# Routing stage of a mixture-of-experts kernel: four input blocks and twelve weight buffers in place of two and four, four weight parts split between the norm's steps

## The reference, cut to what matters

```
xn = (x - mean) / sqrt(var + 1e-5)
attn: v = xn @ Wv.T; r = sigmoid(xn @ Wr.T); wkv = scan over time with decay and first   # no k in it
      (r * wkv) @ Wo.T
ffn:  scores = softmax(xn @ gate_w.T + gate_b)           # 8 experts
      top_w, top_i = top_k(scores, 2)
      y = sum over the 2 chosen experts e of top_w * ((silu(xn @ w1[e].T + b1[e]) * (xn @ w3[e].T + b3[e])) @ w2[e].T + b2[e])
      z = (silu(xn @ ws1.T + bs1) * (xn @ ws3.T + bs3)) @ ws2.T + bs2
out = x + attn(xn) + y + z
```

## Time and profile before

| | |
|---|---|
| median of three runs | 557.25 us (554.65 to 558.19) |
| profiled execution | 556.1 us, span 554.0 us |
| PE busy | 471.2 us (85%) |
| DVE busy | 435.1 us (79%) |
| ACT busy | 234.7 us (42%) |
| POOL busy | 266.9 us (48%) |
| `route` | 0 to 102.4 us of the span |
| first gather of `run_experts` | 102.7 us |

### The profile page before, as it was taken

One profiled execution on the slowest core, in us unless ns is written; L12 is line 12 of the kernel. 1 busy time (PEld: TensorE's weight loads), 2 busy tenths in 40 slices (PEclk: granted clock), 3 DMA queues, 4 the chain that ended last, 5 costly groups with the idle time before them and its releaser, 6 DMA issues. The chain is left out here.

```text
span 554.0 us, 10837 instructions
## 1 busy us (share of the span) xinstructions
PE 471.2 (85%) x2624; PEld 381.1 (69%) x2625; DVE 435.1 (79%) x963; ACT 234.7 (42%) x535; POOL 266.9 (48%) x312
## 2 busy tenths in 40 slices
PE   0668027499999999999999995989999999999997
PEld 0333013188878777777878784777889888988887
DVE  7877869357888888877888873899979696887974
ACT  0335334136656565555655563342232323242321
POOL 6000000353666666666565654878683754657300
PEclk9999555589999999999999998999999999999999
DMA  2798344138434333333333333924471817163111
GB/s 78 258 316 310 122 142 147 28 107 267 124 106 125 111 120 116 114 110 117 104 114 114 104 96 115 321 77 131 125 204 45 236 46 211 58 188 96 58 38 39
DMA packets 58553, 73.95 MB, mean 133 GB/s; under 512 B 6848, under 2 KB 47552, under 8 KB 58528
## 3 DMA queue, kind: packets, MB, share of 16 engines
q1 hardware_dynamic: 52048, 55.94, 30.8%
q0 software_dynamic: 6480, 17.70, 12.0%
HBM read 45.39 MB, written 28.18 MB: 133 GB/s over the span
## 5 line engine op out<-in xcount | busy, mean ns | idle before, releaser
L858 POOL DMA_INDIRECT xg<-xn_rows,picked x71 | 71.1, 1002 | 57.6 <-POOL picked L855 33.3
L1343 POOL DMA_INDIRECT yg<-expert_rows,rows x64 | 72.2, 1128 | 23.6 <-issue 17.1
L855 POOL COPY picked<-tile_tok 128x1 int32 (+1 forms) x71 | 13.9, 196 | 97.8 <-POOLq L315 93.2
L922 PE MATMUL ps_g<-w_hi,x_hi 128*128 x142 | 57.2, 403 | 0.9 <-DVE x_lo L1077 0.9
L922 PE MATMUL ps_g<-w_lo,x_hi 128*128 x142 | 56.6, 398 | 0.0
L922 PE MATMUL ps_g<-w_hi,x_lo 128*128 x142 | 56.5, 398 | 0.0
L1374 PE MATMUL ps_w<-col_hi,s_hi 128*128 128x512 f32 x128 | 51.1, 399 | 1.3 <-DVE res L1569 0.9
L1151 DVE RECIPROCAL rden<-den 128x128 f32<-128x128 f32 x32 | 30.3, 948 | 26.5 <-POOL den L872 26.5
L1375 PE MATMUL ps_w<-col_lo,s_hi 128*128 128x512 f32 x128 | 50.2, 392 | 0.0
L1376 PE MATMUL ps_w<-col_hi,s_lo 128*128 128x512 f32 x128 | 50.2, 392 | 0.0
L995 ACT ACTIVATE act<-ps_g 128x256 f32<-128x256 f32 x71 | 27.2, 383 | 52.0 <-PE ps_g L925 48.5
(11 more groups left out here) (199 smaller groups left out, 1421.8 us busy)
## 6 DMA issues: line engine op xcount, KB each, us to landing
expert_rows<-y SPq DMA_DIRECT2D x71, 128.0 KB
table<-mix_tables SPq DMA_DIRECT2D x16, 384.0 KB
raw_s<-x SPq DMA_DIRECT2D x16, 256.0 KB, 3.7
col<-xn_columns SPq DMA_DIRECT2D x8, 512.0 KB, 7.4
mix_tables<-coef SPq DMA_DIRECT2D x16, 256.0 KB
res<-x SPq DMA_DIRECT2D x16, 256.0 KB
out<-res SPq DMA_DIRECT2D x16, 256.0 KB
xn_rows<-raw_s SPq DMA_DIRECT2D x8, 256.0 KB, 3.7
```

The source lines that it names most:

```text
L858: pool.indirect_dma_start(out=xg[a.buf(NG)][:], out_offset=None, in_=xn_d[:, :], in_offset=bass.IndirectOffsetOnAxis(ap=picked[a.buf(NG)][ ...
L922: nc.tensor.matmul(out, x[:, k, :], w[:, ds(e, 1), k, cols].rearrange("p o n -> p (o n)"), start=(k == 0 and n == 0), stop=False)
L1343: pool.indirect_dma_start(out=yg[a.buf(2)][:, k, q, :], out_offset=None, in_=y_d[:, :], in_offset=bass.IndirectOffsetOnAxis(ap=picked[a.bu ...
```

## The change

- `route` gets buffers of its own: four for `xin` (NX = 4), two for `xn`, two for `xT`, four more of 128 x 768 floats named `w_soon`, and seven for the maps of the choice. The memory of the later stages is allocated after `route` has freed its own, from the other side of SBUF.
- SP loads the first four x blocks at once and behind them weight parts 0 to 3 into `w_soon`. In steps 0 to 3 it loads x block i+4 once `xn` of step i is written; in steps 4 to 7 it loads weight parts 4 to 7 into `xin` buffers that are free by then. Parts 8 and 9 go to `xn`, 10 and 11 to `xT`, 12 to 15 to `w_soon` again.
- ACT clears `bias_hl` in eight pieces of 128 x 768, one after the copies of each step, in place of the memset of POOL.
- DVE does `measure` of step i+1 before `norm` of step i, and splits parts 0 to 3 after the norms of steps 4 to 7; ACT splits them in steps 2 to 5.
- The slot loop has one split per batch on DVE, and one on ACT in its first four batches, behind `hot_tok` and not ahead of it.
- The loops of hardware (`Fori`) in `route` are written out.

```diff
-            w_hi = sb("w_hi", [P, E, KC, WALL], F32R, experts)
...
+            y = [sb(f"y{b}", [P, C], F32, experts, "right") for b in range(2)]
+            w_hi = sb("w_hi", [P, E, KC, WALL], F32R, experts, "right")
...
-        xin = [spare_x[:, b, :].rearrange("p (q c) -> p q c", q=Q) for b in range(2)]
-        xn = [spare_n0, spare_n1[:].rearrange("p k n -> p (k n)").rearrange("p (q c) -> p q c", q=Q)]
-        xT = [spare_t, sb("xT1", [P, KC, STEP], F32)]
-
-        NW = 4
-        w_raw = [t[:].rearrange("p k n -> p (k n)")[:, 0:WALL] for t in (spare_n0, spare_n1, *xT)]
+        NX = 4
+        xin = [sb(f"xin{b}", [P, Q, C], F32) for b in range(NX)]
+        xn = [sb(f"xn{b}", [P, Q, C], F32) for b in range(2)]
+        xT = [sb(f"xT{b}", [P, KC, STEP], F32) for b in range(2)]
+
+        SOON = 4
+        NW = SOON + NX + 4
+        w_soon = [sb(f"w_soon{b}", [P, WALL], F32) for b in range(SOON)]
+        w_raw = ([t[:] for t in w_soon]
+                 + [t[:].rearrange("p k n -> p (k n)")[:, 0:WALL] for t in (*xin, *xn, *xT)])
...
@@ SyncE @@
-                load_x(At(0, 1, 2))
+                for i in range(1, NX):
+                    load_x(At(0, i, NSTEP))
+                for i in range(SOON):
+                    load_w(i)
+
+                def step(a):
+                    sp.wait_ge(s_xn, a.i + 1)
+                    if a.i + NX < NSTEP:
+                        load_x(a.plus(NX))
...
+                    if a.i + NX >= NSTEP:
+                        load_w(SOON + a.i + NX - NSTEP)
...
-                with sp.Fori(1, E * KC // NW) as u:
-                    for r in range(NW):
-                        load_w(At(u, r, NW))
+                for i in range(NW, E * KC):
+                    load_w(i)
...
@@ GpSimd @@
-                nc.gpsimd.memset(bias_hl[:].rearrange("h e n -> h (e n)").bitcast(F32), 0.0).then_inc(s_bzero, 1)
...
@@ ScalarE @@
+                    nc.scalar.activation(bias_hl[:, a.i, :].bitcast(F32), ident[:, 0:1].broadcast_to([P, WALL]),
+                                         ACT.Copy, scale=0.0).then_inc(s_bzero, 1)
...
+                for i in range(1, NSTEP - 2):
+                    step(At(0, i, NSTEP))
+                    if i > 1:
+                        split(i - 2)
...
+                split(SOON)
+                split(SOON + 1)
                 exps(1, EARLY, NSTEP)
-                half = E * KC // 2
-                for n in range(half):
-                    split(At(0, n, half))
+                for i in range(SOON + 2, NW):
+                    split(i)
                 for n in range(PAIRS // BATCH):
-                    if n < half:
-                        split(At(1, n, half))
...
+                    if NW + n < E * KC:
+                        split(NW + n)
...
@@ VectorE @@
+                measure(At(0, 0, NSTEP))
+                for i in range(NSTEP):
+                    if i + 1 < NSTEP:
+                        measure(At(0, i + 1, NSTEP))
+                    norm(At(0, i, NSTEP))
+                    if i > 1:
+                        take(At(0, i - 2, NSTEP))
+                    if i >= NSTEP - SOON:
+                        split(i - NSTEP + SOON)
...
                 for n in range(EARLY, NSTEP):
-                    take(At(n // 2, n % 2, 2))
+                    if n >= NSTEP - 2:
+                        take(At(0, n, NSTEP))
                 choose(1, EARLY, NSTEP)
...
-                split(0)
-                split(1)
+                split(SOON)
+                split(SOON + 1)
...
-                split(2)
+                split(SOON + 2)
+                split(SOON + 3)
...
-                SPLIT_AFTER = [(3, 4), (5, 6), (7,), (8,), (9, 10), (11, 12), (13,), (14, 15)]
+                SPLIT_AFTER = [(8,), (9,), (10,), (11,), (12,), (13,), (14,), (15,)]
```

More of the change, by code:

```diff
@@ new lines, in build @@
+            w_hi = sb("w_hi", [P, E, KC, WALL], F32R, experts, "right")
+            w_lo = sb("w_lo", [P, E, KC, WALL], F32R, experts, "right")
+            bias_hl = sb("bias_hl", [P, E, WALL], F32R, experts, "right")
+            ones2 = sb("ones2", [P, P], F32R, experts, "right")
+            route(nc, x, first, decay, vec_tf, vec_td, gate_w, gate_b, w_all, b_all, xn_d, xT_d, ident, slots, gates,
+                  tile_tok, tile_exp, w_hi, w_lo, bias_hl, ones2)
+            raw_s13 = sb("raw_s13", [P, KC, 2 * SF], F32)
@@ new lines, in build @@
+            raw_s2 = sb("raw_s2", [P, KS, C], F32)
+            raw_o = sb("raw_o", [P, KC, C], F32)
+            vr_hi, vr_lo = (sb(f"vr_{s}", [P, KC, 2 * C], F32R) for s in ("hi", "lo"))
+            col0 = sb("col0", [P, KC, STEP], F32)
+            col_hi0 = sb("col_hi0", [P, KC, STEP], F32R)
+            col_lo0 = sb("col_lo0", [P, KC, STEP], F32R)
+            vec_b1 = sb("vec_b1", [P, KS], F32)
+            vec_b3 = sb("vec_b3", [P, KS], F32)
+            row_b2 = sb("row_b2", [P, C], F32)
@@ L174, in build @@
+            raw_vr = sb("raw_vr", [P, KC, 2 * C], F32, experts, "right")
+            run_experts(nc, xn_d, y_d, y, y_stored, tab_d, vec_tf, vec_td, ident, tile_tok, tile_exp, w_hi, w_lo, bias_hl,
                         ones2,
@@ L188, in route @@
 def route(nc, x, first, decay, vec_tf, vec_td, gate_w, gate_b, w_all, b_all, xn_d, xT_d, ident, slots, gates,
-          tile_tok, tile_exp, w_hi, w_lo, bias_hl, ones2, spare_x, spare_n0, spare_n1, spare_t):
+          tile_tok, tile_exp, w_hi, w_lo, bias_hl, ones2):
     with ExitStack() as ctx:
@@ L230, in route @@
         logits = sb("logits", [P, NT, E], F32)
[L231 to L234, removed]
+        score = maps[0][:].rearrange("p (j e) -> p j e", e=E)
+        work = maps[1][:].rearrange("p (j e) -> p j e", e=E)
+        work2 = maps[2][:].rearrange("p (j e) -> p j e", e=E)
+        hot = [maps[3 + k][:].rearrange("p (j e) -> p j e", e=E) for k in range(TOPK)]
         red = sb("red", [P, NT], F32)
@@ L273, in route @@
         s_small = sem("s_small")
-        s_xin = [sem(f"s_xin{b}") for b in range(2)]
+        s_xin = [sem(f"s_xin{b}") for b in range(NX)]
         s_w = [sem(f"s_w{b}") for b in range(NW)]
@@ L740, in _, with run_experts @@
                                         ).then_inc(s_tok, 1)
-def run_experts(nc, xn_d, y_d, y_stored, tab_d, vec_tf, vec_td, ident, tile_tok, tile_exp, w_hi, w_lo, bias_hl, ones2,
+def run_experts(nc, xn_d, y_d, y, y_stored, tab_d, vec_tf, vec_td, ident, tile_tok, tile_exp, w_hi, w_lo, bias_hl, ones2,
                 cuts, loads):
@@ L765, in run_experts @@
         h_lo = [sb(f"h_lo{b}", [P, KC, P], F32R) for b in range(2)]
-        y = [sb(f"y{b}", [P, C], F32) for b in range(2)]
         s_p = sb("s_p", [P, KC, PIECE + 1], F32)
```

150 lines of the change are left out of this document (42 added, 108 removed).

## The result

The changed kernel takes 569.39 us (median of 4 runs, 568.1 to 571.75), the kernel before in the same job 556.44 us (median of 4 runs, 554.65 to 558.19): a ratio of 1.0238 with a 95% interval of 1.0186 to 1.0289. Forecast were 541 us and a range of 535 to 548. The profiled execution took 570.31 us (before 556.1) with a span of 568.6 us (before 554.0) and a mean granted clock of 0.919 (before 0.941).

A forecast was written before the change was run, and what follows sets the result against it. `route` was taken to set the end, since the first gather waits for its barrier. Start -4.6, norm -1.4, choice and places +0.1, slot loop -10.0 sum to -15.9 us: 541 us, range 535 to 548.

The forecast's parts named there:

- What bounds the kernel: The first gather waits for the barrier behind `route`, so each microsecond by which `route` ends earlier comes off the end.
- Part 1: Start of `route`: without POOL's memset DVE's cast is faster, first BN_STATS at 6.0 in place of 10.62 us, -4.6 us.
- The bound of 0: Start of `route`: no gain, first BN_STATS still at 10.6 us, if the cast is slow for a reason besides the memset.
- Part 2: Norm in `route`: choice starts at 42.7 in place of 48.67 us, -6.0 us, of which 4.6 come from the start.
- one `take` 0.2 us: Norm, DVE's time per step: the copy of logits priced at 0.2 us, six of them in a 40.7 us total.
- the chain from the end of `norm` i over ACT, 5.5 us: Norm: transposes, gate product, logits, piece, split and root take 5.5 us; `norm` i+2 starts about 7 us later, 1.5 spare.
- The transfers of Part 2: Norm, one queue: 11.9 MB ahead of the `xn` store of step 5, 34.6 us at 341 to 345 GB/s; done by 39.4.
- Part 3: Choice to slot loop: earlier `take` saves 0.75 us, one more split costs 0.87, net +0.1; loop starts at 65.4 us.
- Part 4: Slot loop: eight batches with one split each on DVE take 20.4 in place of 30.4 us, -10.0 us.
- The rivals: Norm gains nothing (0.17, 547 us); better case (0.14, 537 or 538); PE at low level (0.04, 566); change hidden (0.03, 557).
- PE falls to its low level: Norm: PE's clock drops between waits for transfers, steps take 7.2 us against 4.1, kernel at 566 us; chance 0.04.
- the signs of being wrong: Clock of 0.5 across the norm, `norm` waiting for `xn_rows` over 2 us in most steps, or other durations after the barrier.

The follow-up runs named there:

- the first experiment: The changed kernel with DVE copying the logits of step i-3, not i-2, after the norm of step i: 540.41 us, ratio 0.971 to the kernel before.
- the last: The first experiment with each `xn` store issued ahead of the next x block and split 3 ahead of the norm's last `take`: 538.20 us, ratio 0.9656.
- the experiment on the memset: The first experiment with `bias_hl` cleared by one memset on POOL again, not by eight pieces on ACT: 544.54 us in one run.

## Why the prediction was wrong

- **What bounds the kernel: right.** `route` sets the end: the span moved with the first gather, by +14.6 us for +13.83 in the change, -15.0 for -15.28 in the first experiment and -15.4 for -16.91 in the last, whose profiled execution was the slowest of its six (540.31 us).
- **Part 1: right.** First BN_STATS at 5.89 us, forecast 6.0. The bound of 0, a cast that is slow for another reason, fell with the experiment on the memset.
- **Part 2: the step that failed is "one `take` 0.2 us".** I priced the moved `take` by its duration and gave it no wait. It waits 5.4 us on average (32.5 / 6), and `norm` of the next block, on which PE waits, stands behind it. I had seen that the change calls `take(i-2)`, and named it a gain: "releases the `back` of step 7 earlier". I went through the chain from the end of `norm` i over ACT, 5.5 us, and compared it with the start of `norm` i+2. That holds for ACT, but asks nothing of DVE's own waits: the logits of i-2 stand on PE behind the transposes of i and the gate product of i-1, and their reader now stands between `norm` i and `norm` i+1. The waits of before don't name it, as `take` of i-3 waited 2.0 us in all. But its price stood in the earlier trace rows, once the two programs are laid side by side: transposes and gate product 1.09 + 1.88 us, and 0.66 us for `back`, which the same trace has on PE though no row of mine showed it. That is 3.6 us, the wait measured at the high level (3.59 us).
- **The transfers of Part 2: right, as soon as the wait is gone.** In the first experiment the norms start at 10.12, 13.66, 18.89, 23.60, 27.54, 32.05, 36.55 and 39.02 us, forecast 10.2, 13.9, 18.6, 23.1, 27.7, 32.5, 37.3 and 40.0, and the choice at 42.49, forecast 42.7. That the choice agrees to 0.2 us is partly luck: the last norm came 1.0 us early, and a wait of 1.12 us for PE ahead of the last `take`, which the forecast lacked, made up for it. The rate of 345 GB/s was set too low: 362 to 379 were reached.
- **Part 3: right.** Choice to loop 22.18 us, forecast 22.7. Here the earlier `take` did bring what I had hoped: with it put back in the first experiment, the same stretch takes 23.62 us.
- **Part 4: right.** 20.28 us, forecast 20.4.
- **The rivals.** None had this mechanism. "PE falls to its low level" (0.04, 566 us) came near in its time and not in its cause: it had PE fall by itself from waits for transfers, with a step of 7.2 us. The fall is the consequence of the wait for DVE, its steps took 10.1 us, and with the order repaired the same transfers leave the clock at 1.00. The rival that had to end on the slower side was sought in the clock and not in the program order, where `measure`, `take` and the splits are moved. Of the signs of being wrong, the low clock in the norm came in part (0.67 from 26 to 36 us); the waits for `xn_rows` didn't.

Three of the sum's four terms are right to 0.5 us; the norm's has the wrong sign. Forecast were -1.4 us from the first BN_STATS to the choice, and measured are +29.1 (67.15 us in place of 38.05); at the choice that is +24.4 us in place of -6.0.

## What to carry to other kernels

When a step is moved on an in-order engine, ask of each of its instructions who must have finished before it and what stands ahead of *that* on the other engine; a copy of 0.2 us that comes one step earlier in a software pipeline can cost a whole pass of the other engine in each step. Two engines that work by turns show themselves in the waits as a wait in both directions in nearly every step (DVE for PE 32.5 us and PE for DVE 21.7 us here, and 1.9 and 6.0 us with the order repaired); leave out the wait before the first step, which every order has. PE's low clock was here for the most part a result of such waits, and it came back to 1.00 when the order was mended, with nothing else done; so look at the order first.

## What the runs showed of the hardware

- A cast of 128 x 128 from int32 to f32 on DVE took 1.13 us, and 6.29 us with a memset of 5.22 us on POOL beside it; it ended 0.23 us behind the memset's end (8.87 against 8.64 us). The Trainium skill (Advanced Engine Details and Errata, section on GPSIMD details) says that the two engines share a read and a write interface, with conflicts for some kinds of DVE instruction. The runs agree in that the cast is slow only beside the memset; that the interface is the reason no run shows.
- The norm's stream of loads and stores together moved up to 387 to 393 GB/s over 10 us, and in the run with the weight parts spread over the steps up to 404, more than the 341 of the earlier trace rows, which I had taken for the full rate.
- The length of a gap alone doesn't tell whether PE's clock falls. From 20 us on it stayed at 1.00 with gaps of up to 1.22 us in the first experiment, of 1.65 us in the run with extra transposes, and once of 2.46 us in the run with spread parts (at 33.47 us; the four gate products behind it took 1.88 us). It fell behind gaps of 2.52 and 2.50 us in the run with extra transposes, and behind 2.02 us in the one with `back` first, where it was 0.50 from 28 to 30 us. Behind gaps of the same 3.08 us it was kept once (in the change at 75.11 us, 1.88 us for four gate products) and lost once (with extra transposes at 67.26 us, 3.42 us for them). In the change the transposes took 1.97 us in place of 1.10 behind each gap from 2.65 to 4.70 us ahead of them.
- In the slot loop PE was at 0.50 for 20 us on end in every kernel, in the change though busy for 17.69 of 20 us with bf16 products. What keeps it there was not tried.
